# A graph network kernel: convolutions by half tiles, a third gather buffer, spread groups, and the final pass's loads on ScalarE's queue

## What is computed

```python
edge_index = jnp.stack([src, dst])
x = _layernorm(x + _L0_gnn_ref(x, edge_index, W, att_src, att_dst, bias), axis=-1)
x = _layernorm(x + _L1_gnn_ref(x, src, dst, thetas, phis, gammas, betas), axis=-1)

# attention layer (8 heads of 32)
h = jnp.einsum('nf,fhd->nhd', x, W)
e = leaky_relu(a_src[src] + a_dst[dst], 0.2)
alpha = exp(e - segment_max(e, dst)[dst]) / segment_sum(e_exp, dst)[dst]
out = relu(segment_sum(h[src] * alpha, dst) + bias)

# convolution, for each of 3 layers
e = relu((x[dst] - x[src]) @ thetas[l].T + x[src] @ phis[l].T)
agg = segment_max(e, src, num_segments=N), 0 where a node has no edge
x = relu((agg - mu) * rsqrt(var + 1e-5) * gammas[l] + betas[l])
```

## Time and profile before

| | |
|---|---|
| median of three runs | 1758.32 us |
| profiled execution, device time | 1768.92 us |
| its span in the trace | 1767.1 us |
| VectorE busy | 1239.4 us (70%) |
| TensorE busy | 1076.6 us (61%) |
| ScalarE busy | 985.7 us (56%) |
| GpSimd busy | 955.6 us (54%) |
| moved by DMA | 431.98 MB, 244 GB/s over the span |

### The profile page before, as it was taken

One profiled execution on the slowest core, in us unless ns is written; L12 is line 12 of the kernel. 1 busy time (PEld: TensorE's weight loads), 2 busy tenths in 40 slices (PEclk: granted clock), 3 DMA queues, 4 the chain that ended last, 5 costly groups with the idle time before them and its releaser, 6 DMA issues.

```text
span 1767.1 us, 16600 instructions
## 1 busy us (share of the span) xinstructions
PE 1076.6 (61%) x3823; PEld 562.5 (32%) x3823; DVE 1239.4 (70%) x2657; ACT 985.7 (56%) x2630; POOL 955.6 (54%) x1013
## 2 busy tenths in 40 slices
PE   0139888781004661699999699997999987000000
PEld 0023333330002331455555355554545544000000
DVE  8847877678978994255455355563666678989998
ACT  4735877665455775244444455564555453766665
POOL 1047756667767777777777677524544137640000
PEclk9999999895557876799999899998999999555555
DMA  9276899988694674588886589856866359999999
GB/s 366 101 227 214 284 324 354 334 306 257 222 294 157 202 228 144 155 261 264 255 269 203 120 187 202 184 162 122 153 141 134 84 186 309 420 412 389 383 404 366
DMA packets 174965, 431.98 MB, mean 244 GB/s; under 512 B 28308, under 2 KB 107682, under 8 KB 154900
## 3 DMA queue, kind: packets, MB, share of 16 engines
q1 hardware_dynamic: 107748, 227.24, 37.0%
q0 software_dynamic: 43904, 98.91, 22.9%
q10 hardware_dynamic: 23216, 104.77, 16.8%
HBM read 254.11 MB, written 180.72 MB: 246 GB/s over the span
## 4 chain that ended last, share of the span: by engine, by line
PE 42%; DMA 20%; DVE 20%; issue 6%; POOL 5%; ACT 4%; SPq 2%; ACTq 0%; POOLq 0%; DVEq 0%
PE ps L1296 14%; PE ps L1309 14%; DMA out<-arena 10%; PE ps L1286 4%; DMA arena<-x 3%; DMA x_dst<-arena 3%; DVE stat L806 2%; PE ps L1473 2%; PE ps L1325 2%; PE ps L887 2%; DMA arena<-x,idx 2%; POOL x L1162 2%; ACT arena L845 2%; DVE arena L1068 2%; DVE arena L803 2%
## 5 line engine op out<-in xcount | busy, mean ns | idle before, releaser
L1381 DVE TENSOR_TENSOR_SCAN arena<-arena,ps 128x512 f32<-128x512 f32 (+1 forms) x150 | 186.7, 1253 | 242.5 <-PE ps L1296 209.2
L860 POOL DMA_INDIRECT arena<-x,idx x196 | 186.1, 949 | 182.5 <-DVE idx L622 90.8
L1267 POOL DMA_INDIRECT arena<-agg,slot x196 | 185.3, 945 | 181.4 <-PE ps L1286 80.4
L1309 PE MATMUL ps<-arena 128*128 128x512 f32 x600 | 269.5, 592 | 10.5 <-ACT arena L1351 10.5
L1296 PE MATMUL ps<-arena 128*128 128x512 f32 x600 | 270.1, 593 | 0.0
L1242 POOL DMA_INDIRECT arena<-x,idx x196 | 185.6, 947 | 61.0 <-issue 57.0
L1578 ACT ACTIVATE ps<-arena 128x256 f32<-128x256 f32 x391 | 143.7, 367 | 96.4 <-DVE arena L1550 96.4
L845 ACT ACTIVATE arena<-arena,shift,inv 128x256 f32<-128x256 f32 (+1 forms) x311 | 156.1, 589 | 50.9 <-DVE shift L837 34.2
L1385 DVE TENSOR_TENSOR ps<-arena,ps 128x512 f32<-128x512 f32 (+1 forms) x150 | 101.7, 683 | 96.6 <-PE ps L1309 96.3
L1351 ACT ACTIVATE arena<-big,bn_shift,bn_scale 128x512 f32<-128x512 f32 (+1 forms) x100 | 75.1, 798 | 162.1 <-PE ps L1309 150.3
L1309 PEld LDWEIGHTS ps<-arena 128*128 128x128 f32 x600 | 115.5, 193 | 151.5 <-issue 139.9
(11 more groups left out here) (214 smaller groups left out, 2166.9 us busy)
## 6 DMA issues: line engine op xcount, KB each, us to landing
arena<-x SPq DMA_DIRECT2D x39, 1280.0 KB, 9.3
out<-arena SPq DMA_DIRECT2D x39, 1280.0 KB, 11.8
arena<-x ACTq DMA_DIRECT2D x31, 1280.0 KB, 10.5
x<-arena ACTq DMA_DIRECT2D x31, 1280.0 KB, 6.4
agg<-arena SPq DMA_DIRECT2D x48, 512.0 KB, 4.1
arena<-not_same SPq DMA_DIRECT2D x72, 256.0 KB
arena<-last_of SPq DMA_DIRECT2D x72, 256.0 KB
x_dst<-arena SPq DMA_DIRECT2D x24, 512.0 KB, 3.6
```

The costliest lines, as they stand in the source:

```text
L860: pl.indirect_dma_start(rows_in[:, par, a, g, :], None, x[:, :], bass.IndirectOffsetOnAxis(ap=idx[:, k, t * G + g:t * G + g + 1], axis=0)) ...
L1267: pl.indirect_dma_start(conv_in[:, b, 1, g, :], None, agg_dram[l - 1][:, :], bass.IndirectOffsetOnAxis(ap=slot[:, t * G + g:t * G + g + 1] ...
L1309: m = pe.matmul(near_bank[j][:, 0:width(t)], thp[:, l, 1, k, j * P:(j + 1) * P], near_t[:, par, k, 0:width(t)], start=(k == 0), stop=(k == 1))
L1381: v.tensor_tensor_scan(runmax[:, par, j, 0:width(t)], mask[:, tl % 2, 0:width(t)], far_bank[j][:, 0:width(t)], initial, ALU.add, ALU.max). ...
```

## The change

- **Third buffer.** Target rows of the attention stage have three buffers (`DST_RING`), source rows still two. The waits are parted: target gather t waits for the target half of turn(t-3) and the store of tile t-3, source gather t for turn(t-2).
- **Spread groups.** The eight groups in `big` are no longer 4 to 11 but stand at tile steps 0, 3, 5, 8, 11, 13, 15 and 18; ring groups stand between them. `pre_node_rows` gives each the rows that its place was loaded with.
- To make room, `msq` and `tiles_f` lie in the tensor `score`.
- **Convolutions by halves.** In layer 0 PE's order is: turn target half of t, near(t-1), turn source half of t, rows(t-2), far(t). In layers 1 and 2: four dummy products, near(0), five dummy products, turn(0), far(0), turn(1), far(1), near(1), and from there as before. ScalarE copies the rows of a tile a step earlier in layer 0, and in layer 1 copies the last tile's rows ahead of its squares; SyncE stores results behind the mask loads of the same step, and the last ones ahead of the last mask load.
- **Final pass.** ScalarE's queue issues the loads: the first four when the last squares are done, load t just ahead of the activations of tile t. SyncE has no part in the final pass and goes straight to the dense stage, whose first four loads so stand beside it.

```diff
-        s_dst_got = [sem("dst_got_0"), sem("dst_got_1")]
+        DST_RING = 3
+        s_dst_got = [sem(f"dst_got_{b}") for b in range(DST_RING)]
...
+        rows_dst_3 = sb("rows_dst_3", [P, G, D])
...
+        BIG_STEPS = (0, 3, 5, 8, 11, 13, 15, 18)
+        BIG_GROUPS = [PRE_SORT + k for k in BIG_STEPS]
+        RING_GROUPS = [g for g in range(PG + 1) if g not in BIG_GROUPS]
+        assert len(BIG_STEPS) == PRE_BIG
 
         def in_big(g):
 
-            return PRE_SORT <= g < PRE_SORT + PRE_BIG
+            return g in BIG_GROUPS
...
             for t in range(NS):
-                par = t % 2
+                if t >= DST_RING:
+                    pl.wait_ge(s_row_turned, 4 * (t - DST_RING) + 2)
+                    pl.wait_ge(s_xd_stored[t % DST_RING], 16 * (t // DST_RING))
+                for g in range(cols(t)):
+                    pl.indirect_dma_start(dst_rows(t)[:, g, :], None, x[:, :],
+                                          bass.IndirectOffsetOnAxis(ap=idx[:, D_DST, t * G + g:t * G + g + 1], axis=0)).then_inc(s_dst_got[t % DST_RING], 16)
                 if t > 1:
                     pl.wait_ge(s_row_turned, 4 * (t - 1))
-                    pl.wait_ge(s_xd_stored[par], 16 * (t // 2))
...
-            first = 2 if l else 0
-            for s in range(first, NS + 3):
-                if l < L - 1 and 0 <= s - 3:
-                    store(s - 3)
-                if s < (NS + 2 if l < L - 1 else NS):
-                    masks(s)
+            lag = 2 if l == 0 else 3
+            for s in range(2 if l else 0, NS):
+                masks(s)
+                if l < L - 1 and s >= lag:
+                    store(s - lag)
             if l < L - 1:
+                masks(NS)
+                for t in range(NS - lag, NS):
+                    store(t)
+                masks(NS + 1)
...
+            def keep_clock(count):
+                pe.wait_ge(s_conv_scan, 2 * NS * l)
+                for _ in range(count):
+                    pe.matmul(far_bank[0], ident[:, :], thp[:, l, 0, :, :].rearrange("p k f -> p (k f)"), start=True, stop=True)
...
-            if l:
-                near(0)
-            in_steps([(0, turn), (1, products)] + ([(2, rows)] if l < L - 1 else []), NS)
+            if l == 0:
+                for t in range(NS):
+                    turn(t, False)
+                    if t > 0:
+                        near(t - 1)
+                    turn(t, True)
+                    if t > 1:
+                        rows(t - 2)
+                    far(t)
+                near(NS - 1)
+                rows(NS - 2)
+                rows(NS - 1)
+                return
+            keep_clock(4)
+            near(0)
+            keep_clock(5)
+            turn(0, False)
+            far(0)
+            turn(1, False)
+            far(1)
+            near(1)
+            for s in range(2, NS + 2):
+                if s < NS:
+                    turn(s, False)
+                if 2 < s <= NS:
+                    far(s - 1)
+                    near(s - 1)
+                if l < L - 1:
+                    rows(s - 2)
...
-        def final_sync(sp):
-            sp.wait_ge(s_conv_squared, 2 * NS * L)
+        def final_act(a):
+            def fin_load(t):
+                if t >= FX:
+                    a.wait_ge(s_fin_sum, t - FX + 1)
+                a.dma_start(fin_x[:, t % FX, 0:cols(t), :], x1s_dram[edges(t), :].rearrange("(g p) f -> p g f", p=P)).then_inc(s_fin_x[t % FX], 16)
+            a.wait_ge(s_conv_squared, 2 * NS * L)
+            for t in range(FX):
+                fin_load(t)
+            a.wait_ge(s_bn_ready, L)
             for t in range(NS):
                 if t >= FX:
-                    sp.wait_ge(s_fin_sum, t - FX + 1)
-                sp.dma_start(fin_x[:, t % FX, 0:cols(t), :], x1s_dram[edges(t), :].rearrange("(g p) f -> p g f", p=P)).then_inc(s_fin_x[t % FX], 16)
...
+                    fin_load(t)
...
             for l in range(L):
                 conv_sync(sp, l)
-            final_sync(sp)
             dense_sync(sp)
```

More of the change, by code:

```diff
@@ L734, in pre_store @@
         def pre_store(a, g):
-            rows, p, r = node_rows(g)
-            stored = s_big_stored[g - PRE_SORT] if in_big(g) else s_rows_stored[ring_use(g) % PRE_RING]
+            rows, p, r = pre_node_rows(g)
+            stored = s_big_stored[BIG_GROUPS.index(g)] if in_big(g) else s_rows_stored[ring_use(g) % PRE_RING]
             a.wait_ge(s_pre_normed, g + 1)
@@ L846, in pre_norm, with dst_rows, src_rows @@
             m.then_inc(s_pre_normed, 1)
+        def dst_rows(t):
+            b = t % DST_RING
+            return rows_dst_3 if b == 2 else rows_in[:, b, 1, :, :]
+        def src_rows(t):
+            return rows_in[:, t % 2, 0, :, :]
         def gat_pool(pl):
@@ L869, in turn @@
                     a, j = 1 - n // 2, n % 2
-                    if j == 0:
-                        pe.wait_ge((s_src_got, s_dst_got)[a][t % 2], 16 * cols_landed(t, 2))
+                    if n == 0:
+                        pe.wait_ge(s_dst_got[t % DST_RING], 16 * cols_landed(t, DST_RING))
+                    if n == 2:
+                        pe.wait_ge(s_src_got[t % 2], 16 * cols_landed(t, 2))
+                    rows = dst_rows(t) if a else src_rows(t)
                     if t:
@@ L1273, in conv_pe, with turn @@
                 pe.wait_ge(s_x1_sum, NC)
[L1275 removed]
+            def turn(t, near_rows):
                 b = t % RC
[L1277 to L1278 removed]
+                if near_rows:
+                    pe.wait_ge(s_near_got[b], 16 * cols_landed(t, RC))
+                else:
+                    pe.wait_ge(s_far_got[b], 16 * far_landed(l, t))
+                for n in (2, 3) if near_rows else (0, 1):
                     a, j = 1 - n // 2, n % 2
[L1280 to L1281 removed]
                     use = turns_before(l, t) + n
@@ L1310, in near @@
                     m.then_inc(s_near_done, 1)
-            def products(t):
-                far(t)
-                if l == 0 or t:
-                    near(t)
+            def keep_clock(count):
+                pe.wait_ge(s_conv_scan, 2 * NS * l)
+                for _ in range(count):
+                    pe.matmul(far_bank[0], ident[:, :], thp[:, l, 0, :, :].rearrange("p k f -> p (k f)"), start=True, stop=True)
             def rows(t):
@@ L1370, in keep_rows @@
                     a.activation(agg_rows[:, par, 2 * b:2 * b + 2, :].rearrange("p g f -> p (g f)"), row_bank[b], ACT.Copy).then_inc(s_agg_kept, 1)
-            in_steps([(0, keep)] + ([(3, keep_rows)] if l < L - 1 else []) + [(2, squares)], NS)
+            for s in range(NS + 2):
+                if s < NS:
+                    keep(s)
+                if l == 0 and s >= 2:
+                    keep_rows(s - 2)
+                if l == 1 and s >= 3:
+                    keep_rows(s - 3)
+                if l == 1 and s == NS + 1:
+                    keep_rows(NS - 1)
+                if s >= 2:
+                    squares(s - 2)
         def conv_dve(v, l):
```

63 lines of the change are left out of this document (29 added, 34 removed).

## The result

The changed kernel takes 1845.62 us (median of four runs, 1840.88 to 1847.89) against 1761.98 for the kernel before (median of four): ratio 1.0448, 95% interval 1.0409 to 1.0487. It is slower, as forecast, but by 83.6 us where I had 41; the time lies above the range (1765 to 1835). The profiled execution took 1840.88 us (span 1839.0, 71.9 more than the span of before).

The account below looks back on a forecast made before the run. No engine bounds the whole kernel; each stage was read alone. Attention -24, convolutions -17, final pass +97, last stage -15 sum to +41 us, applied to the median 1758.32: 1799 us, range 1765 to 1835.

Parts of the forecast that it names:

- the loop: Final pass: load waits for the sum four tiles back, ahead of activations, means, subtraction, sum; 97 us more, between 80 and 114.
- the step of 7.5 us: Final pass: time per tile, taken between 6.6 and 8.3 us, against 2.76 before; 20 tiles give 95 us.
- Rival (b): Final pass: PE's clock stays at the lower level throughout, step 8.3 us, 16 us more, 1815 us; chance 15%.
- All 32 us could go: Attention stage: GpSimd's waits for target-row stores could vanish with the third buffer; 24 us taken, between 8 and 32.
- the slack of 8 us: Before layer 0: VectorE's and ScalarE's chain may come forward 8 us less, and attention-stage gains still reach the first gather.
- The bound of 4.7 us by the slot lookups: Layer 0's end: layer 1's gathers cannot begin before 977.3 us, behind 20 slot lookups, so 4.7 us won.
- The terms 5.8, 5.1 and 1.5: Convolutions: far(1) starts 5.8 us earlier in layer 1, 5.1 in layer 2; earlier last-row copy and store in layer 1, 1.5.
- I bounded it by VectorE (253 us): Last stage: VectorE's 6.1 us per group, 39 groups, gaps and last stores make 253 us against 273; 15 won taken.
- (a): Final pass: the wait holds only the load, not the activations; 2.76 us per tile stays, 1704 us, faster; chance 9%.
- (c): Attention stage: the DMA engines are full (share 96%) and the third buffer gives 8 us, so 1815 us; chance 12%.
- (d): Whole kernel: clock holds, every gain comes full, 1764 to 1785 us; chance 5% within 0.5% of before, 9% above it.
- (e): Last stage: the dense loads' waits could keep even group 0 behind the sums; left inside the range (13 us), no chance given.

Follow-up runs that it names:

- clock_held: The changed kernel with three extra products of 512 columns (results unused) behind each turn of the final pass from tile 4 on: 1817.81 us, ratio 1.0289.

## Why the prediction went wrong, point by point

By the two profiles it missed 31 us: 71.9 where it had 41. The convolutions are 13.1 of them (3.9 won, 17 forecast), the final pass 12.6, the attention stage 5.8 (18.2 won, 24 forecast), and the last stage came as forecast. So the loop, which decides the sign, was right in its mechanism and its step mis-sized; the gains of the convolutions were worked out for the wrong instruction.

**Final pass: mechanism right, one term too small.** The wait in front of the activations closed the loop, each link as listed. The failed number is the step of 7.5 us, taken midway between 6.6 (full clock, which clock_held measured at 6.58) and 8.3 (low clock, of which steps of 8.27 occur). It was 8.1 in the mean; twenty steps of 0.6 us more are the 12 by which the pass outgrew the forecast (109.6 against 97). The midpoint had no row behind it: the earlier trace rows showed the low level after a single gap of 3.2 us, and here PE idles 4 us of 6.6 in every step. Rival (b) deserved more than 15%.

**Attention stage: 24 forecast, about 13.5 got.** The profile pair shows 18.2 at the first gather of layer 0. But the mean over the three executions with two buffers and the old order is 700.3, over the ten with three buffers 686.8. The first step that failed is "All 32 us could go", with 24 taken of it. The wait for stores did go (35.2 to 4.2), but 4.9 to 17.6 us of waiting for PE stand in the ten executions (0 to 1.7 in the three), and the 35.2 was itself a high draw (29.5 and 26.0 in the two others). At the last gather 18.1 us are left in the mean (371.6 to 353.5). The second is the slack of 8 us, by which all of it should have reached layer 0: another 4.6 are gone there. GpSimd's waits for ScalarE's normalised rows, ahead of its puts, are 4.8 to 8.0 us in the ten and were 1.5 to 4.6 in the three, 3.9 more in the mean; in the profile pair ScalarE's last such row came 16.4 us earlier (691.3 to 674.9) where the last gather came 20.8.

**Convolutions: 17 forecast, 4 got.** The bound of 4.7 us by the slot lookups was right: layer 0 gave 5.1 in the mean. The terms 5.8, 5.1 and 1.5 did not arrive: layers 1 and 2 took 437.3 us in the mean, 436.4 with the old order. I followed far(1) and stopped there; the next in PE's order, tile 3's turning in layer 1, waits for rows that GpSimd issues behind four lookups, and in layer 2 tile 0's turning waits behind five extra products, which I had called free "until rows arrive".

**Last stage: 15 forecast, 15.6 got, mechanism right.** I bounded it by VectorE (253 us). VectorE is busy 243.3 of the 257.4 us, and it waits for loads 4.2 us in all, where it waited 18.3 in the kernel before. Its waits in the last stage, changed kernel, then before:

```profile
DVE arena L1625 <- DMA arena<-x: 4.2, 5, 1.4
```
```profile
DVE arena L1550 <- DMA arena<-x: 18.3, 20, 3.5
```

The four loads and 41 of the 53 puts were gone before the stage began. The DMA engines are at 0.98 here too, so little was left on that side either. The 15 itself was a choice between 6 and 20.

**Sum.** By the profile pair: -22.1 ahead of the final pass (41 forecast), +109.6 (97), -15.6 (15) = +71.9. The medians say 83.6. The missing 11.7 are how the two profiled executions lie in their sets: that of before 6.9 above its median (1768.92 against 1761.98; it began the final pass 5 us later than the mean of three, 1414.0), that of the changed kernel 4.7 below its own (1840.88 against 1845.62).

**The rivals.** (a) is refuted: ScalarE waited 140.6 us behind the load. (b) came close: ten of the twenty steps took 8.25 us or more. (c), full DMA engines in the attention stage, did not decide: the share is 0.88 from 99 to 356 us, not 0.96. (d) is out: neither the clock nor the gains held. (e) did not happen: SyncE issues the first dense load at 1421.4, and VectorE's first dense addition starts at 1581.5, directly behind the last sum.

## What to carry to other kernels

A DMA issued from a computing engine puts its wait in front of that engine's next computation: place it where its condition has long been met, or leave it to an engine that computes nothing. Transfers moved to an earlier stage are a gain only if the DMA engines idle there, so read their share over both stages together. And follow a microsecond won to the next instruction that waits for something else: here it was lost a few instructions on, both times. Last, before a second placement is measured, write out the order of instructions that it gives: here two edits that look different gave the same one.

## What was not expected of the hardware

Products added to PE's order, their results unused, made a stage faster: 63 more products, 28 us less, since the granted clock went from 0.72 to 0.96. The same device at the start of layer 2 cost time. And with one and the same code in these two stages (nine executions) the DMA engines at a share of 0.94 or 0.95 moved 355 to 369 GB/s from one execution to another, which makes up to 14 us over the last two stages; what sets that rate is open.
